# Two normalisation chains moved ahead in a three-engine schedule: GpSimd's second normalisation before its row DMAs, VectorE's and ScalarE's attention statistics, normalisation and residual before the low halves

## The chip, the cores and the metric

The kernel runs on one core of a Trainium2 chip. Its five engines (TensorE, VectorE, ScalarE, GpSimd and SyncE, in the profile PE, DVE, ACT, POOL and SP) each work through their own list of instructions in order, and are tied together by semaphores alone: an instruction that waits holds back all that is behind it on its engine. The metric is the device time of one execution in microseconds (us), the median of several runs; less is better.

## What is computed

One block of a sandwich network over x of shape (16, 1024, 256), float32: an attention-like gated recurrence, then a mixture of eight experts with a common overflow network. Both have a normalisation in front, one behind, and a residual sum. Cut to what matters:

```python
# first half, per sequence of 1024 tokens
n = layernorm(x)
g = sigmoid(n @ Wg.T + bg)
h_t = (1 - g_t) * h_(t-1) + g_t * n_t          # recurrence along the sequence
x = x + layernorm(h @ Wo.T + bo)
# second half, tokens of all sequences in one row
xf = layernorm(x)
eid = argmax(softmax(xf @ router_w + router_b))  # one of 8 experts
rank = how many earlier tokens chose the same expert
if rank < 320:  y = relu(xf @ w1[eid] + b1[eid]) @ w2[eid] + b2[eid]
else:           y = relu(xf @ ow1 + ob1) @ ow2 + ob2   # overflow network
x = x + layernorm(y)
```

## The kernel before

The 16,384 tokens are cut into 32 groups of 512 (NG = 32), two to a sequence; a group is named (i, v), with v = 0 or 1 its half. A loop of 32 steps runs over them, written as two steps u = 0 and u = 1 in a hardware loop, with the first and the last steps written out. It is a software pipeline. Step (i, u) works on `now`, for which it computes the routing and the overflow network (all tokens go through it), on `nxt`, the group after, for which it finishes the first half up to the transposed, normalised input of the second, and on `far`, the group after that, for which it does the first normalisation, the gate matmuls and the recurrence. Steps 0 to 30 have a `nxt`, steps 0 to 29 a `far`. Behind the loop eight experts are computed from rows that the steps scattered to DRAM (`xbuf`), 320 rows each; the change does not touch that part.

Matmuls are in float32 split into a high and a low half, three products for one: ScalarE makes the high half by a copy that rounds, VectorE (or GpSimd, for `hst_lo`) the low half by a subtraction. The hidden layer of 1024 is worked in eight slices j of 128. For each there are `layer1(j)` on TensorE (six matmuls into `psH`), `relu(j)` on ScalarE (the relu into `hid`, line 540, and the copy into `hid_hi`, line 544), `lo(j)` on VectorE (`hid_lo`, line 834), and `layer2(j)` on TensorE (twelve matmuls into `psY`). `low(j)` in VectorE's step is `lo(now, j)`, and `hidden(range)` in ScalarE's step is `relu` for those j.

The order of each engine within a step is written out by hand. TensorE's (lines 1116 to 1146) is: layer1(0), route, layer1(1), logits; project(nxt); layer1(2), layer2(0); layer1(3), layer2(1), transposes0(far); layer1(4), rank(now), layer2(2); layer1(5), layer2(3), **gate(far)**; layer1(6), layer2(4); layer1(7), layer2(5); **transposes1(nxt)**; layer2(6), layer2(7). The other engines' steps of before are in the listing below; their pieces are:

- `attended(nxt)` (VectorE, line 753) takes the projection out of PSUM into `att`. `stats1` takes its mean and variance (`read_rows`, four bn_stats, line 701, and `moments`, four bn_aggr, line 708, and two small tensor_scalar instructions, lines 712 and 713). `deviation(1)` on GpSimd makes `rstd` and `nmr` of them (lines 362 and 364), `norm1` on ScalarE normalises `att` in place (line 550), and `residual1` on VectorE adds x and writes `x1` (line 769).
- `stats2(nxt)` takes mean and variance of `x1`, `norm2` on GpSimd (with its `deviation(2)`) writes the normalised `tok2` (line 403, shown as tok), and `transposes1` on TensorE (line 1065) turns it into `psT`, from which `xf_hi` and `xf_lo` make the input of the next step.
- `choose(now)` finds the expert of each token from the logits. `rank(now)` on TensorE counts earlier tokens with the same expert, into `ranks`, which lies in `psA`; `place(now)` on VectorE (lines 816 to 829) turns that into a row number, `idx`, and signals `s_idx`; `dispatch(now)` on GpSimd issues four indirect DMAs (line 383) that write the rows of `x1` to `xbuf`.
- `norm0(far)` (GpSimd, tok, line 373), `transposes0`, `xn_hi` (ScalarE) and `xn_lo` (VectorE, line 734) make the input of the gate matmuls; `sigmoid(far)` and `recurrence(far)` follow them.
- `residual2(prev)` on GpSimd (line 438) is the last sum of the group before, 128x1024 in one instruction; SyncE stores it.

The gate matmuls write `psA`. Their waits, on TensorE, are on both halves of their input, on `attended(nxt)`, and on the row numbers of the group two before `far`, which is `now`:

```python
def gate(g):
    pe.wait_ge(s_xn_hi, cnt(g, 2, 2))
    pe.wait_ge(s_xn_lo, cnt(g, 2, 2))
    ...
    prev = grp(g[0], g[1], -2)
    if live(prev, NG):
        pe.wait_ge(s_idx, cnt(prev, 1, 1))
```

Of the kernel before, what the change touches and what calls it, by code (L numbers as in the profile page):

```python
# [14 lines left out]
D = 256  # L15
# [5 lines left out]
TG = 4  # L21
# [15 lines left out]
def cnt(g, n, k):  # L37
    return g[0] * (2 * n) + (g[1] * n + k)
# [8 lines left out]
def live(g, n):  # L47
    return not isinstance(g[0], int) or 0 <= 2 * g[0] + g[1] < n


def sandwich_kernel(nc, x, Wg, bg, Wo, bo, router_w, router_b, w1, b1, w2, b2, ow1, ob1, ow2, ob2, out):
    B, L, _ = x.shape
    N = B * L
    NG = N // GT
# [3 lines left out]
    with ExitStack() as ctx:  # L58
# [56 lines left out]
        x1 = [sb(f"x1_{v}", [P, TG, PITCH]) for v in range(2)]  # L115
# [79 lines left out]
        s_x1 = sem("s_x1")  # L195
# [143 lines left out]
        def _(pool):  # L339
# [47 lines left out]
            def renumber(g):  # L387

                i, v = g
                if live(grp(i, v, -2), NG):  # L390
                    pool.wait_ge(s_scat[v], landed(grp(i, v, -2), TG))
                    pool.sem_inc(s_held, 1)
                    pool.tensor_scalar(x1[v][:, :, D:ROW], x1[v][:, :, D:ROW], float(2 * GT), None, ALU.add)\
                        .then_inc(s_id, 1)

            def norm2(g, src, n, base=0):
                i, v = g
                deviation(2, g, n, base)
                pool.wait_ge(s_nm[2], cnt(g, 1, 1) + base)
                pool.wait_ge(s_T1, cnt(g, 2, 0) + 2 * base)  # L400
                pool.sem_inc(s_held, 1)
                for t in range(n):
                    last = pool.tensor_scalar(tok2[:, t, :], src[v][:, t, 0:D], rstd[2][:, t:t + 1],  # L403
                                              nmr[2][:, t:t + 1], ALU.mult, ALU.add)
                last.then_inc(s_tok2, 1)
# [9 lines left out]
            def step(i, u):  # L415
                prev, now, nxt, far = grp(i, u, -1), grp(i, u, 0), grp(i, u, 1), grp(i, u, 2)
                if live(prev, NG):
                    deviation(3, prev, TG)
                if live(far, NG):
                    norm0(far)  # L420
                if live(prev, NG):
                    residual2(prev)
                if live(nxt, NG):
                    deviation(1, nxt, TG)
                    renumber(nxt)
                if live(now, NG):
                    dispatch(now, range(TG))
                if live(nxt, NG):
                    norm2(nxt, x1, TG)
                if live(far, NG):  # L430
                    state_lo(far)

# [93 lines left out]
        def _(act):  # L526
# [19 lines left out]
            def norm1(g):  # L546
                act.wait_ge(s_nm[1], cnt(g, 1, 1))
                act.wait_ge(s_att, cnt(g, 2, 2))
                for t in range(TG):
                    last = act.activation(att[:, t, :], att[:, t, :], ACT.Identity, bias=nmr[1][:, t:t + 1],  # L550
                                          scale=rstd[1][:, t:t + 1])
                last.then_inc(s_u, 1)
# [53 lines left out]
            def step(i, u):  # L606
                now, nxt, far = grp(i, u, 0), grp(i, u, 1), grp(i, u, 2)
                run, up, ahead = live(now, NG), live(nxt, NG), live(far, NG)

                def hidden(js):  # L610
                    if run:
                        for j in js:
                            relu(now, j, GT, biasT[:, OB1 + j:OB1 + j + 1])

                hidden(range(0, 1))
                if run:
                    logits_out(now)
                hidden(range(1, 2))
                if live(grp(i, u, -1), NG):
                    norm3(grp(i, u, -1), TG)  # L620
                hidden(range(2, 4))
                if ahead:
                    xn_hi(far)
                hidden(range(4, 5))
                if up:
                    norm1(nxt)
                if not ahead:
                    for j in range(4 * u, 4 * u + 4):
                        weights_hi((0, 0), j)
                hidden(range(5, 6))  # L630
                if ahead:
                    sigmoid(far)
                hidden(range(6, 8))
                if up:
                    xf_hi(nxt, GT)
                if ahead:
                    state_hi(far)
# [56 lines left out]
        def _(dve):  # L694
# [21 lines left out]
            def stats(k, src, g, n, base=0):  # L716

                read_rows(k, src, n)
                moments(k, g, n, base)
# [39 lines left out]
            def stats1(g):  # L759
                dve.wait_ge(s_att, cnt(g, 2, 2))  # L760
                stats(1, lambda t: att[:, t, :], g, TG)

            def residual1(g):
# [4 lines left out]
                dve.wait_ge(s_u, cnt(g, 1, 1))  # L768
                dve.tensor_tensor(x1[v][:, :, 0:D], att[:], xin[v][:], ALU.add).then_inc(s_x1, 1)

            def stats2(g):
                dve.wait_ge(s_x1, cnt(g, 1, 1))
                stats(2, lambda t: x1[g[1]][:, t, 0:D], g, TG)

            def xf_lo(g, n, base=0):
                for c in range(DC):
# [92 lines left out]
            def step(i, u):  # L869
                now, nxt, far = grp(i, u, 0), grp(i, u, 1), grp(i, u, 2)  # L870
                run, up, ahead = live(now, NG), live(nxt, NG), live(far, NG)

                def low(*js):
                    if run:
                        for j in js:
                            lo(now, j, GT)

                low(0, 1)
                if run:
                    choose(now)  # L880
                if up:
                    attended(nxt)
                low(2)
                if up:
                    stats1(nxt)
                low(3)
                if ahead:
                    xn_lo(far)
                if run:
                    place(now)  # L890
                low(4)
                if up:
                    residual1(nxt)
                    stats2(nxt)
                low(5)
                if ahead:
                    recurrence(far)
                else:
                    for j in range(4 * u, 4 * u + 4):
                        weights_lo((0, 0), j)  # L900
                low(6)
                next_x = grp(i, u, 3)
                if live(next_x, NG):
                    read_rows0(next_x)
                low(7)
                if up:
                    xf_lo(nxt, GT)
                if live(next_x, NG):
                    moments(0, next_x, TG)
                if run and not up:  # L910
                    read_rows2((0, 0))
                    moments(2, (0, 0), ET, NG)
                if run:
                    result(now, ob2_b[:].unsqueeze(1), TG)
                if run and not up:
                    xf_lo((0, 0), C, NG)
                if run:
                    stats3(now, TG)
# [292 lines left out]
```

## Time and profile before

| | us |
|---|---|
| median of 3 runs | 1307.19 |
| lowest and highest run | 1305.34, 1312.45 |
| span of the profiled execution | 1305.6 |
| the profiled execution's own time beside its span | not given by the page |
| mean granted clock of TensorE over the span (share of 2.4 GHz) | 0.971 |

The first step starts at about 51.5 us and the last ends at about 1142 us; ahead of them lies the preparation of the weights, behind them the experts. A profile row gives the engine and the line of the kernel that issued the instruction, what it writes and reads, and its duration; in a timeline the first number is the start in us and the second the time to the end of the last of the merged instructions, and a bracket gives the idle time of the engine ahead of it and what ended that. Two instructions of one engine can overlap by some tenths of a microsecond, since they are pipelined.

### The profile page before, as it was taken

To read this page: it belongs to the slowest core of one execution; us is meant where nothing else is said; L and a number is where in the kernel's file an instruction comes from. 1 tells how busy PE (TensorE), PEld (TensorE's weight loads), DVE (VectorE), ACT (ScalarE), POOL (GpSimd) and SP (SyncE) were. 2 spreads that over 40 slices of the span, in tenths; PEclk is the share of its full clock that TensorE was granted. 3 is DMA by queue.
4 is the path that set the end of the run, shared out by engine and by line. 5 is a ranking of instruction groups with operands and counts; after the bars stand their busy time and mean duration, and the time that the engine had idled before them with its cause. 6 is when DMAs were issued, how large, how long until landed. Compare 5 with 4: busy or idle time off the path is not lost. (4 is left out here: it accounts for less than half of the span.)

```text
span 1305.6 us, 24820 instructions
## 1 busy us (share of the span) xinstructions
PE 1182.1 (91%) x7705; PEld 1048.7 (80%) x7705; DVE 1005.7 (77%) x2731; ACT 773.7 (59%) x1362; POOL 807.3 (62%) x887
## 2 busy tenths in 40 slices
PE   5599999999999999999999999999999999889994
PEld 4388888888888888888888888888888888789994
DVE  5678888887788878787888788787878776578892
ACT  4366566665656656665655556656655565467773
POOL 4466666666666666666666666656666665336774
PEclk9799999999999999999999999999999999989997
DMA  8211111111011010110111100101010100334430
GB/s 235 81 34 49 50 46 43 39 35 32 32 32 32 32 32 32 32 32 16 32 32 32 32 22 27 32 32 32 32 32 32 32 16 18 101 102 152 144 119 31
DMA packets 59687, 65.32 MB, mean 50 GB/s; under 512 B 7835, under 2 KB 55885, under 8 KB 59524
## 3 DMA queue, kind: packets, MB, share of 16 engines
q1 hardware_dynamic: 52484, 59.58, 14.6%
q0 software_dynamic: 7168, 5.32, 1.3%
q8 instruction: 16, 0.26, 0.1%
q14 instruction: 19, 0.16, 0.0%
HBM read 40.17 MB, written 38.87 MB: 61 GB/s over the span
## 5 line engine op out<-in xcount | busy, mean ns | idle before, releaser
L540 ACT ACTIVATE hid<-psH,biasT 128x512 f32<-128x512 f32 (+1 forms) x320 | 209.4, 654 | 281.0 <-PE psH L1011 257.8
L362 POOL TENSOR_TENSOR rstd<-veps,mhalf 128x4 f32<-128x4 f32 (+1 forms) x144 | 193.2, 1342 | 266.6 <-DVE nmean L713 266.3
L1109 PE MATMUL psY<-W_hi,hid_hi 128*128 128x256 f32 x1216 | 355.4, 292 | 0.9 <-DVE hid_lo L834 0.9
L1111 PE MATMUL psY<-W_lo,hid_hi 128*128 128x256 f32 x1216 | 348.0, 286 | 0.0
L1112 PE MATMUL psY<-W_hi,hid_lo 128*128 128x256 f32 x1216 | 347.9, 286 | 0.0
L834 DVE TENSOR_TENSOR hid_lo<-hid,hid_hi 128x512 fp32r<-128x512 f32 (+1 forms) x320 | 262.7, 821 | 99.1 <-ACT hid_hi L544 93.6
L1009 PE MATMUL psH<-xfT_hi,W_hi 128*128 128x512 f32 (+1 forms) x640 | 246.0, 384 | 6.2 <-ACT hid L540 3.4
L1109 PEld LDWEIGHTS psY<-W_hi,hid_hi 128*128 128x128 f32 x1216 | 235.1, 193 | 10.5 <-DVE hid_lo L834 1.8
L1011 PE MATMUL psH<-xfT_hi,W_lo 128*128 128x512 f32 (+1 forms) x640 | 242.7, 379 | 0.0
L1010 PE MATMUL psH<-xfT_lo,W_hi 128*128 128x512 f32 (+1 forms) x640 | 242.4, 379 | 0.0
L1111 PEld LDWEIGHTS psY<-W_lo,hid_hi 128*128 128x128 f32 x1216 | 234.3, 193 | 6.7
L1112 PEld LDWEIGHTS psY<-W_hi,hid_lo 128*128 128x128 f32 x1216 | 234.1, 192 | 0.0
L544 ACT ACTIVATE hid_hi<-hid 128x512 fp32r<-128x512 f32 (+1 forms) x320 | 192.2, 601 | 10.2
L383 POOL DMA_INDIRECT xbuf<-x,idx x128 | 140.9, 1101 | 89.8 <-DVE idx L829 55.0
L1009 PEld LDWEIGHTS psH<-xfT_hi,W_hi 128*128 128x128 f32 x640 | 121.8, 190 | 24.8 <-ACT hid L540 4.2
L1011 PEld LDWEIGHTS psH<-xfT_hi,W_lo 128*128 128x128 f32 x640 | 121.6, 190 | 22.5
L412 POOL TENSOR_TENSOR hst_lo<-hst,hst_hi 128x512 fp32r<-128x512 f32 x64 | 82.1, 1304 | 85.9 <-ACT hst_hi L582 85.9
L1010 PEld LDWEIGHTS psH<-xfT_lo,W_hi 128*128 128x128 f32 x640 | 121.9, 190 | 14.5
L1065 PE MATMUL psT<-ident,tok 128*128 128x128 f32 x304 | 46.8, 302 | 82.8 <-POOL tok L403 82.8
L1065 PEld LDWEIGHTS psT<-ident,tok 128*128 128x128 f32 x304 | 36.3, 151 | 91.0 <-POOL tok L403 89.3
L589 ACT ACTIVATE xfT_hi<-psT 128x512 fp32r<-128x512 f32 (+1 forms) x80 | 41.8, 562 | 106.6 <-PE psT L1065 106.5
L778 DVE TENSOR_TENSOR xfT_lo<-psT,xfT_hi 128x512 fp32r<-128x512 f32 (+1 forms) x80 | 49.1, 645 | 68.7 <-ACT xfT_hi L589 68.1
(110 smaller groups left out, 2290.6 us busy)
## 6 DMA issues: line engine op xcount, KB each, us to landing
xin<-L_attn_x SPq DMA_DIRECT2D x32, 512.0 KB
stage<-L_ffn_w SPq DMA_DIRECT2D x16, 1024.0 KB, 6.3
out<-outt SPq DMA_DIRECT2D x32, 512.0 KB, 2.9
xbuf<-zrow SPq DMA_DIRECT2D x1, 2570.0 KB, 17.7
xin<-xbuf SPq DMA_DIRECT2D x8, 257.0 KB, 5.7
stage<-L_ffn_ow SPq DMA_DIRECT2D x2, 1024.0 KB, 10.8
xbuf<-x,idx POOLq DMA_INDIRECT x128
b_b<-L_ffn_b SPq DMA_DIRECT2D x1, 1024.0 KB, 14.1
```

The costliest lines, as they stand in the source:

```text
L362: pool.tensor_tensor(rstd[k][:, 0:n], veps[k][:, 0:n], mhalf[:, 0:n], ALU.pow).then_inc(s_rs[k], 1)
L383: pool.indirect_dma_start(out=xbuf, out_offset=bass.IndirectOffsetOnAxis(idx[v][:, t:t + 1], 0), in_=x1[v][:, t, 0:ROW], in_offset=None, b ...
L540: act.activation(hid[j % 2][:, 0:n], psH[:, j % 2, 0:n], ACT.Relu, bias=bias).then_inc(s_hid, 1)
L544: act.activation(hid_hi[j % 4][:, 0:n], hid[j % 2][:, 0:n], ACT.Copy).then_inc(s_hid_hi, 1)
L834: dve.tensor_tensor(hid_lo[j % 4][:, 0:n], hid[j % 2][:, 0:n], hid_hi[j % 4][:, 0:n].bitcast(F32), ALU.subtract).then_inc(s_hid_lo, 1)
L1009: pe.matmul(dst, w_hi, r_hi, start=(k == 0), stop=False)
L1010: pe.matmul(dst, w_hi, r_lo, start=False, stop=False)
L1011: return pe.matmul(dst, w_lo, r_hi, start=False, stop=(k == last_k))
L1065: last = pe.transpose(psT[:, c, t * P:(t + 1) * P], tok2[:, t, c * P:(c + 1) * P], ident[:])
L1109: pe.matmul(psY_t[:, t, :], hi, w[0][:, j, :], start=(j == 0 and t % 2 == 0), stop=False, skip_group_check=True)
L1111: pe.matmul(psY_t[:, t, :], hi, w[1][:, j, :], start=False, stop=False, skip_group_check=True)
L1112: last = pe.matmul(psY_t[:, t, :], lo_, w[0][:, j, :], start=False, stop=(j == HC - 1), skip_group_check=True)
```

## The change

GpSimd's step computes `norm2(nxt)` before `dispatch(now)`. ScalarE's step runs `norm1(nxt)` ahead of `xn_hi(far)` and relu 4, not behind them. VectorE's step takes the attention statistics before low(2), then low(2) and low(3), then `residual1` and the four bn_stats of `x1`, then `xn_lo(far)`, then the moments of `x1`, low(4) and low(5), and only then `place(now)`. `stats2` is split into `read_rows2a` and `moments` so that `xn_lo` can stand between. TensorE's and SyncE's orders are as they were.

```diff
--- before.py
+++ after.py
@@ -423,10 +423,9 @@
                 if live(nxt, NG):
                     deviation(1, nxt, TG)
                     renumber(nxt)
+                    norm2(nxt, x1, TG)
                 if live(now, NG):
                     dispatch(now, range(TG))
-                if live(nxt, NG):
-                    norm2(nxt, x1, TG)
                 if live(far, NG):
                     state_lo(far)
 
@@ -619,11 +618,11 @@
                 if live(grp(i, u, -1), NG):
                     norm3(grp(i, u, -1), TG)
                 hidden(range(2, 4))
+                if up:
+                    norm1(nxt)
                 if ahead:
                     xn_hi(far)
                 hidden(range(4, 5))
-                if up:
-                    norm1(nxt)
                 if not ahead:
                     for j in range(4 * u, 4 * u + 4):
                         weights_hi((0, 0), j)
@@ -768,9 +767,13 @@
                 dve.wait_ge(s_u, cnt(g, 1, 1))
                 dve.tensor_tensor(x1[v][:, :, 0:D], att[:], xin[v][:], ALU.add).then_inc(s_x1, 1)
 
+            def read_rows2a(g):
+                dve.wait_ge(s_x1, cnt(g, 1, 1))
+                read_rows(2, lambda t: x1[g[1]][:, t, 0:D], TG)
+
             def stats2(g):
-                dve.wait_ge(s_x1, cnt(g, 1, 1))
-                stats(2, lambda t: x1[g[1]][:, t, 0:D], g, TG)
+                read_rows2a(g)
+                moments(2, g, TG)
 
             def xf_lo(g, n, base=0):
                 for c in range(DC):
@@ -880,19 +883,18 @@
                     choose(now)
                 if up:
                     attended(nxt)
-                low(2)
+                    stats1(nxt)
+                low(2, 3)
                 if up:
-                    stats1(nxt)
-                low(3)
+                    residual1(nxt)
+                    read_rows2a(nxt)
                 if ahead:
                     xn_lo(far)
+                if up:
+                    moments(2, nxt, TG)
+                low(4, 5)
                 if run:
                     place(now)
-                low(4)
-                if up:
-                    residual1(nxt)
-                    stats2(nxt)
-                low(5)
                 if ahead:
                     recurrence(far)
                 else:
```

## Rows read from the trace of the kernel before

**Rows 1.** The page, part 1: busy time, share, instructions.

```profile
PE 1182.1 (91%) x7705; PEld 1048.7 (80%) x7705; DVE 1005.7 (77%) x2731; ACT 773.7 (59%) x1362; POOL 807.3 (62%) x887
```

**Rows 2.** TensorE's waits, 60 to 1110 us: total, times, longest (us).

```profile
PE psT L1065 <- POOL tok L403: 60.7, 31, 3.2
```

**Rows 3.** Windows, logits copy to logits copy: length, busy PE, PEld, DVE, ACT, POOL, clock, DMA.

```profile
566.88:602.39 35.51, 33.41 (x211) 29.53 (x210) 27.89 (x77) 20.67 (x37) 22.42 (x24) 0.95 0.09 30
602.39:635.89 33.50, 31.86 (x211) 27.97 (x210) 26.96 (x77) 20.44 (x36) 21.71 (x24) 1.00 0.11 31
635.89:669.87 33.98, 31.87 (x211) 27.98 (x210) 27.74 (x77) 20.56 (x37) 22.46 (x24) 1.00 0.10 31
```

**Rows 4.** Timeline, TensorE, the second transposes: start, duration, instruction, [wait].

```profile
150.79 1.86 PE L1065 MATMUL psT<-ident,tok 128*128 128x128 f32 x8 [1.91 <-POOL tok L403]
...
629.25 1.09 PE L1065 MATMUL psT<-ident,tok 128*128 128x128 f32 x8 [1.64 <-POOL tok L403]
...
1003.74 1.50 PE L1065 MATMUL psT<-ident,tok 128*128 128x128 f32 x8 [2.10 <-POOL tok L403]
...
1140.18 1.54 PE L1065 MATMUL psT<-ident,tok 128*128 128x128 f32 x6 [4.94 <-POOL tok L403]
```

**Rows 5.** Timeline, GpSimd, 599 to 667 us.

```profile
608.44 2.38 POOL L438 TENSOR_TENSOR outt<-ysb,x 128x1024 f32<-128x1024 f32 x1
...
615.12 0.63 POOL L364 TENSOR_TENSOR nmr<-nmean,rstd 128x4 f32<-128x4 f32 x1
...
623.29 1.84 POOL L362 TENSOR_TENSOR rstd<-veps,mhalf 128x4 f32<-128x4 f32 x1
...
642.72 2.41 POOL L438 TENSOR_TENSOR outt<-ysb,x 128x1024 f32<-128x1024 f32 x1
```

**Rows 6.** Timeline, TensorE, around the gate matmuls of two steps.

```profile
617.35 0.39 PE L1011 MATMUL psH<-xfT_hi,W_lo 128*128 128x512 f32 x1
...
619.01 0.39 PE L1009 MATMUL psA<-xnT_hi,WgT_hi 128*128 128x512 f32 x1
...
652.40 0.29 PE L1112 MATMUL psY<-W_hi,hid_lo 128*128 128x256 f32 x1
652.52 0.39 PE L1009 MATMUL psA<-xnT_hi,WgT_hi 128*128 128x512 f32 x1
```

**Rows 7.** Timeline, VectorE, 599 to 667 us.

```profile
606.96 1.27 DVE L756 TENSOR_TENSOR att<-psA,bo_b 128x512 f32<-128x512 f32 x2
...
609.60 1.77 DVE L834 TENSOR_TENSOR hid_lo<-hid,hid_hi 128x512 fp32r<-128x512 f32 x1 [1.37 <-ACT hid_hi L544]
...
613.41 0.16 DVE L713 TENSOR_SCALAR nmean<-mv 128x4 f32<-128x4 f32 x1
...
621.74 0.69 DVE L834 TENSOR_TENSOR hid_lo<-hid,hid_hi 128x512 fp32r<-128x512 f32 x1
...
648.40 1.29 DVE L734 TENSOR_TENSOR xnT_lo<-xnT,xnT_hi 128x512 fp32r<-128x512 f32 x2
```

**Rows 8.** Timeline, ScalarE, 599 to 667 us.

```profile
616.12 2.07 ACT L550 ACTIVATE att<-att,nmr,rstd 128x256 f32<-128x256 f32 x4
...
626.23 0.69 ACT L540 ACTIVATE hid<-psH,biasT 128x512 f32<-128x512 f32 x1 [1.47 <-PE psH L1011]
626.95 0.63 ACT L544 ACTIVATE hid_hi<-hid 128x512 fp32r<-128x512 f32 x1
```

**Rows 9.** Timeline, VectorE, the last step.

```profile
1122.52 0.18 DVE L816 TENSOR_TENSOR rk<-psA,row 128x32 f32<-128x32 f32 x1
...
1123.62 0.17 DVE L829 CAST idx<-slot 128x4 int32<-128x4 f32 x1
...
1127.01 0.69 DVE L834 TENSOR_TENSOR hid_lo<-hid,hid_hi 128x512 fp32r<-128x512 f32 x1 [2.62 <-ACT hid_hi L544]
```

**Rows 10.** Timeline, all engines, 606 to 609 us.

```profile
606.27 2.20 POOL L373 TENSOR_SCALAR tok<-xin,rstd,nmr 128x256 f32<-128x256 f32 x4 [0.29 <-POOL nmr L364]
...
606.34 0.23 DVE L797 SCALAR_TENSOR_TENSOR cand<-lg,first 128x32 f32<-128x32 f32 x1
```

## Prediction

> **What bounds the kernel now.** I read the page's busy shares first, then the waits of TensorE, then the busy time of single steps, then the timeline of two neighbouring steps engine by engine. TensorE is busy 91% of the span, well ahead of VectorE's 77% [rows 1]. From the first step to the last that prepares another group, the trace shows TensorE waiting for one thing only: 31 times for the second normalised tile `tok2`, 60.7 us in all, 1.96 us each [rows 2]. Single steps show the same. Measured from one copy of the logits to the next, TensorE is busy 31.87 us in every step at the full clock; the rest is that wait, 1.63 us in a step with u=0 and 2.11 us in one with u=1 [rows 3]. So a step costs 31.87 us plus TensorE's waits. A third term is in the first of these rows: after some of the 2.1 us waits the clock falls to the lower of its two levels (1.2 instead of 2.4 GHz) for a while, the mean of the step is 0.95, and the same matmuls take 33.41 us, 1.54 us more. Seven of the 16 waits of 1.9 to 2.2 us are followed by this, the first at 150.79 and the last at 1003.74; of the 13 of 1.6 us, as at 629.25, none is [rows 4].
>
> **What the change removes.** GpSimd now computes `tok2` ahead of the four row DMAs, and VectorE has the statistics for it ready earlier. In the step that begins at 599.55 GpSimd starts on it at 623.29, behind the DMAs [rows 5], and TensorE's wait ends at 629.25 [rows 4], 6 us later. In the new order the statistics are there at about 619.8 (below) and nothing of GpSimd's is in front, so `tok2` is done by 625.8; TensorE wants it at 627.6 and, by what follows, later. I take the 31 waits as gone: -60.7 us.
>
> **What it adds: a wait of TensorE in front of the gate matmuls.** `gate(far)` waits on `s_idx` of the present group (line 1033), since it overwrites the PSUM in which `place(now)` reads the ranks. Up to now `place` ran before `low(4)`, and the gate started without a wait, at 619.01 and at 652.52 [rows 6]. The change puts `place` behind `low(5)`, and moves the attention statistics, the whole of `residual1`, the second statistics and `xn_lo` in front of it too. Everything that TensorE still has for this step (layer 1 for j=6 and 7, layer 2 from j=4, the transposes, the next step) is queued behind the gate. So I work out when `place` ends.
>
> First the start of `norm1` on ScalarE. `attended` ends at 608.23. Four statistics and the moments follow; now they run from 611.3, behind `low(2)`, to 613.57, 2.3 us [rows 7], which gives 610.5. But the two small tensor_scalar instructions at their end fall under GpSimd's residual addition, 2.38 us from 608.44, and a VectorE instruction with this kind of access is held by it: `low(2)` took 1.77 us, more than twice the 0.69 us of `low(5)`, and finished 0.55 us after the addition [rows 5, 7]. So the moments end at 611.05. From there to the end of GpSimd's nmr the present chain takes 613.57 to 615.75, 2.2 us, 0.63 of it an nmr with a VectorE `xn_lo` beside it [rows 5, 7]; I take 2.0. `norm1` starts at 613.1. With u=1 the residual addition runs from 642.72 to 645.13 [rows 5], later in its step by 0.8 us; the moments end at 645.4 and `norm1` starts at 647.45.
>
> Then from `norm1` to the end of `place`. From the start of `norm1` through `residual1` and the second statistics to the VectorE instruction behind them the trace has 616.12 to 621.74, 5.62 us [rows 7, 8]; no slack lies in it, since each waits for the one before. In the new order the two `xn_lo` (1.29 us [rows 7]) stand inside this stretch; they hide the 0.16 us between statistics and moments, so about 1.05 us more: 6.7. `low(4)` and `low(5)` follow back to back, 1.2 us for both (two `xn_lo`, of the same shape, take 1.29 with the pipeline's end). Their inputs come later than now, since `norm1` and `xn_hi` are ahead of relu 4 on ScalarE: 613.1 plus some 2 us for each of the two and two pairs of 1.3 us give 619.7, just in time. `place` takes 1.27 us (1122.52 to 1123.79 [rows 9]). Sum: 6.7 + 1.2 + 1.3 = 9.2 us.
>
> So the gate starts at 622.3 instead of 619.01, 3.3 us late, and with u=1 at 656.7 instead of 652.52, 4.15 us late. The last matmul before it ends 0.17 us after the gate could start (652.40 + 0.29 against 652.52 [rows 6]), so idle time as the rows count it is 3.15 and 4.0 us, mean 3.56. 30 steps have a gate: +106.8 us. Against -60.7 that is **+46 us**.
>
> **The last step.** There `place` moves from 1122.5 to behind `low(5)`, which ends at 1127.7 [rows 9], so the last row DMAs start 5.2 us later. The reload of the rows, the expert's normalisation and the transposes, for which TensorE waits 4.94 us already [rows 4], all follow from them: **+5 us**.
>
> **The clock.** None of the waits of 1.6 us is followed by a fall, seven of 16 near 2 us are, and the one of 4.94 us too: the six transposes behind it, started at 1140.18, took 1.54 us, and the eight of 629.25 took 1.09 us [rows 4]. So waits of 3 to 4 us should meet it more often than those of 2. I take 20 of the 30, seven being there already: 13 x 1.54 = **+20 us**. The bounds are no more than now (0) and every step (+35).
>
> **Sum**: 1305.6 + 46 + 5 + 20 = 1377. The page gives the profiled execution's span and no other time of it; the span lies 1.6 us below the median of 1307.2, so I forecast 1378 us.
>
> **VectorE beside GpSimd.** The cost I can bound least is what GpSimd's second normalisation does to `low(4)`, `low(5)` and `place`, with which it now coincides. The long two-input addition holds VectorE [rows 5, 7]. The normalisations don't seem to: `cand` (two inputs in SBUF) took 0.23 us under GpSimd's `tok` [rows 10], against 0.18 us for `rk`, of the same size with one of its inputs in PSUM [rows 9]. I take nothing; the bound above is one wait of half an instruction of `tok` (2.2 us for four [rows 10]) for each of some seven small instructions, 2 us a step, 60 us.
> By the Trainium skill (SBUF — State Buffer, Who interferes with whom) a VectorE instruction with two SBUF inputs and a GpSimd one that reads SBUF exclude each other, and the second is blocked until the first is done. `low(4)`, `low(5)` and three of `place`'s (lines 820, 821 and 823) are such instructions, and GpSimd's `tok` reads SBUF; the rule would bring the sum near the upper bound. The row of `low(2)` agrees with it for the long addition, the row of `cand` does not for `tok`.
>
> **Rivals.**
> 1. Only what can't be avoided is paid. `place` cannot start before `low(5)`: layer 1 for j=5 ends at 617.74 [rows 6], relu and copy take 1.35 us [rows 8], `low(5)` 0.69, `place` 1.27, so the gate starts at 621.1 at the earliest, with 1.95 us idle. That is what is removed (1.96): 30 x 1.95 - 60.7 + 5 = +3, so 1310, with the clock as now. It needs VectorE to be 1.2 to 2 us ahead of my chain, and the chain is made of rows without slack. Chance 0.05.
> 2. Faster. The same floor, and no wait of it is followed by a fall of the clock: 1307 + 3 - 11 = 1299. It decides when all waits stay under about 1.9 us, above which the trace first shows a fall. As the floor itself is 1.95, chance 0.04.
> 3. The gate wait as worked out, but the clock falls no more often than now, or the moments are not held by the addition: 1350 to 1362. In my own range; chance 0.2.
> 4. VectorE is held by the normalisation in small pieces, 0.5 to 2 us a step: 1395 to 1438. For it: the addition of [rows 5]; against it: [rows 10]. Chance 0.14.
> 5. The transposes still wait: `tok2` is ready at 624.5 and TensorE comes at 630.8, so this would take 6 us that I don't see. Chance 0.02.
> The forecast itself, 1362 to 1395, has the rest, 0.55.
>
> **How the numbers follow.** Within 0.5% (6.5 us), about what a measurement of this kernel can tell from no change, is rival 1: 0.05. Faster is rival 2: 0.04. Slower is the rest: 0.91. The range leaves out rivals 1 and 2 and the upper half of rival 4: 1345 to 1412. Its ends are also the sum with the gate wait 0.5 us shorter and few more falls, and the sum with every step's clock falling and 0.6 us of contention.
>
> **What would show it.** In the profile after: no wait of the transposes (line 1065) for `tok`; in its place one of the gate matmuls on `psA` (line 1009) for `idx` of line 829, 30 times, 3 to 4 us, longer with u=1; TensorE busy 31.87 us in a step at full clock; more steps with a clock below 1.00; `norm1` starting some 3 us earlier in the step; `place` last before the recurrence. The prediction is wrong if the gate starts without a wait, if the wait is near 2 us (VectorE ahead of my chain) or above 4.5 us (VectorE held), or if the clock stays at 1.00 through such waits.

## The result and the profile after

The changed kernel takes 1394.2 us (median of 4 runs, 1392.9 to 1397.4) beside 1306.8 us for the kernel before: 1.0665 times as long, 95% interval 1.0638 to 1.0692. It is slower by 87 us, inside the range given and 16 us above the time predicted. Executions of one kernel beside each other agree within 0.8% here, but for one of eight of the kernel with `place` two low halves earlier (1645.6 us, at a mean granted clock of 0.654) and the longer of the two with GpSimd's part undone (1463.8 us), and neither of these enters a ratio.

The page after: busy time and share of each engine.

```profile
PE 1218.2 (87%) x7705; PEld 1073.6 (77%) x7705; DVE 991.7 (71%) x2731; ACT 769.7 (55%) x1362; POOL 756.9 (54%) x887
```

TensorE's share has fallen from 91 to 87% [rows 1], although it is busy 36 us longer with the same 7705 matmuls. Its waits from 60 to 1200 us are these (total, times, longest), where the kernel before had 60.7 us for `tok` alone [rows 2]:

```profile
PE psA L1011 <- DVE idx L832: 107.6, 30, 4.1
PE psT L1067 <- POOL tok L403: 1.7, 1, 1.7
```

The wait for `tok2` is gone but for one step, and a wait of the gate matmuls for `idx` stands in its place, 30 times, 3.6 us on the mean. Three steps, again from one copy of the logits to the next (length; busy PE, PEld, DVE, ACT, POOL; granted clock; DMA):

```profile
280.75:315.97 35.22, 31.89 (x211) 28.04 (x210) 26.21 (x77) 20.42 (x37) 21.16 (x24) 1.00 0.10 32
536.62:573.90 37.28, 33.41 (x211) 29.14 (x210) 27.38 (x77) 20.40 (x36) 20.27 (x24) 0.95 0.09 28
573.90:611.61 37.71, 34.40 (x211) 29.94 (x210) 26.43 (x77) 20.40 (x36) 20.59 (x24) 0.91 0.08 28
```

The first is one of the four steps with a gate in which the clock stays at its upper level: 31.89 us busy, as before [rows 3], and 3.33 us of waiting. The second has one stretch at the lower level and costs 1.52 us more in matmuls. The third has a mean clock of 0.91 and costs 2.5 us more; before, no step went under 0.95. TensorE's timeline around its gate:

```profile
590.41 0.29 PE L1114 MATMUL psY<-W_hi,hid_lo 128*128 128x256 f32 x1
594.01 0.77 PE L1011 MATMUL psA<-xnT_hi,WgT_hi 128*128 128x512 f32 x1 [3.31 <-DVE idx L832]
594.57 0.63 PE L1012 MATMUL psA<-xnT_lo,WgT_hi 128*128 128x512 f32 x1
595.00 0.63 PE L1013 MATMUL psA<-xnT_hi,WgT_lo 128*128 128x512 f32 x1
```

The last matmul in front starts at 590.41, and the gate 3.6 us later. In [rows 6] these two are 0.12 us apart. Two gate matmuls behind it are 0.43 us apart, where at the upper level they are 0.23 us apart: the clock was already down when the wait ended. Half-microsecond windows of TensorE show from when to when (busy time, count, granted clock), here in the step with 0.91 and below it in the one with 0.95:

```profile
592.50:593.00 0.50, 0.00 (x0) 0.72 0.00 0
593.00:593.50 0.50, 0.00 (x0) 0.50 0.00 0
599.00:599.50 0.50, 0.50 (x3) 0.50 0.01 0
599.50:600.00 0.50, 0.50 (x3) 0.96 0.00 0
```

```profile
558.00:558.50 0.50, 0.50 (x3) 1.00 0.00 0
558.50:559.00 0.50, 0.50 (x3) 0.58 0.00 0
561.50:562.00 0.50, 0.50 (x3) 0.51 0.00 0
562.00:562.50 0.50, 0.50 (x4) 1.00 0.06 1
```

In the first the clock is down from 592.7 to 599.5, 6.8 us, 5.5 of them with work; in the second, whose wait ended at 557.3, it falls behind the wait, at 558.6, and is back after 3.4 us.

VectorE, GpSimd and ScalarE in the same step, which begins at 571.06:

```profile
581.78 0.61 DVE L711 TENSOR_SCALAR veps<-mv 128x4 f32<-128x4 f32 x1
...
586.98 1.23 DVE L768 TENSOR_TENSOR x<-att,xin 128x1024 f32<-128x1024 f32 x1 [2.35 <-ACT att L549]
...
589.56 1.28 DVE L733 TENSOR_TENSOR xnT_lo<-xnT,xnT_hi 128x512 fp32r<-128x512 f32 x2
...
591.38 1.29 DVE L837 TENSOR_TENSOR hid_lo<-hid,hid_hi 128x512 fp32r<-128x512 f32 x2
592.59 0.18 DVE L819 TENSOR_TENSOR rk<-psA,row 128x32 f32<-128x32 f32 x1
...
593.69 0.17 DVE L832 CAST idx<-slot 128x4 int32<-128x4 f32 x1
```

```profile
579.98 2.38 POOL L437 TENSOR_TENSOR outt<-ysb,x 128x1024 f32<-128x1024 f32 x1
...
591.56 1.41 POOL L362 TENSOR_TENSOR rstd<-veps,mhalf 128x4 f32<-128x4 f32 x1 [6.55 <-DVE nmean L712]
...
593.56 2.17 POOL L403 TENSOR_SCALAR tok<-x,rstd,nmr 128x256 f32<-128x256 f32 x4 [0.29 <-POOL nmr L364]
```

```profile
584.80 2.08 ACT L549 ACTIVATE att<-att,nmr,rstd 128x256 f32<-128x256 f32 x4 [0.90 <-POOL nmr L364]
```

This is the chain of the prediction, link by link, in a step with u=0. The residual addition (579.98, 2.38 us) holds the small tensor_scalar of the attention moments (0.61 us for 0.17); `norm1` starts at 584.80; `residual1` at 586.98, `xn_lo` at 589.56, low(4) and low(5) at 591.38, `place` at 592.59. Its last instruction ends at 593.86 and the gate starts at 594.01. In a step with u=1 that last instruction falls under GpSimd's `tok`, which starts at 556.56 there, and takes 0.40 us instead of 0.17 us, in all 15 of them:

```profile
556.74 0.40 DVE L832 CAST idx<-slot 128x4 int32<-128x4 f32 x1
```

Behind the steps, the transposes for the first expert wait 9.48 us, where they waited 4.94 us [rows 4]:

```profile
1228.74 1.54 PE L1067 MATMUL psT<-ident,tok 128*128 128x128 f32 x6 [9.48 <-POOL tok L403]
```

### The profile page after: what moved, and what is told of

It is laid out like the page before. It is cut to its first block and busy times, and to the rows that moved or that the text cites. A ratio compares the mean times of both kernels' runs of the same rounds, so it can differ in the third digit from the quotient of the medians.

```text
span 1395.7 us, 24833 instructions
## 1 busy us (share of the span) xinstructions
PE 1218.2 (87%) x7705; PEld 1073.6 (77%) x7705; DVE 991.7 (71%) x2731; ACT 769.7 (55%) x1362; POOL 756.9 (54%) x887
## 5 line engine op out<-in xcount | busy, mean ns | idle before, releaser
L362 POOL TENSOR_TENSOR rstd<-veps,mhalf 128x4 f32<-128x4 f32 (+1 forms) x144 | 179.2, 1245 | 375.4 <-DVE nmean L712 375.4
L1111 PE MATMUL psY<-W_hi,hid_hi 128*128 128x256 f32 x1216 | 350.3, 288 | 1.2 <-DVE hid_lo L837 1.2
L837 DVE TENSOR_TENSOR hid_lo<-hid,hid_hi 128x512 fp32r<-128x512 f32 (+1 forms) x320 | 210.4, 666 | 96.5 <-ACT hid_hi L543 88.7
L1111 PEld LDWEIGHTS psY<-W_hi,hid_hi 128*128 128x128 f32 x1216 | 230.1, 189 | 10.3 <-DVE hid_lo L837 1.9
L1113 PEld LDWEIGHTS psY<-W_lo,hid_hi 128*128 128x128 f32 x1216 | 229.9, 189 | 6.6
L383 POOL DMA_INDIRECT xbuf<-x,idx x128 | 146.2, 1143 | 44.2 <-issue 35.8
L1011 PE MATMUL psA<-xnT_hi,WgT_hi 128*128 128x512 f32 x128 | 71.5, 558 | 110.7 <-DVE idx L832 107.6
L573 ACT ACTIVATE keep<-psA,neg_bg 128x512 f32<-128x512 f32 x64 | 43.9, 688 | 208.2 <-PE psA L1013 208.2
L1011 PEld LDWEIGHTS psA<-xnT_hi,WgT_hi 128*128 128x128 f32 x128 | 33.7, 263 | 124.1 <-issue 116.9
L743 DVE SCALAR_TENSOR_TENSOR xnT<-keep,xnT 128x512 f32<-128x512 f32 x64 | 44.1, 689 | 110.6 <-ACT keep L573 110.2
## 6 DMA issues: line engine op xcount, KB each, us to landing
xbuf<-zrow SPq DMA_DIRECT2D x1, 2570.0 KB, 19.1
b_b<-L_ffn_b SPq DMA_DIRECT2D x1, 1024.0 KB, 14.4
```

Of the source, the lines that this page charges most:

```text
L362: pool.tensor_tensor(rstd[k][:, 0:n], veps[k][:, 0:n], mhalf[:, 0:n], ALU.pow).then_inc(s_rs[k], 1)
L383: pool.indirect_dma_start(out=xbuf, out_offset=bass.IndirectOffsetOnAxis(idx[v][:, t:t + 1], 0), in_=x1[v][:, t, 0:ROW], in_offset=None, b ...
L837: dve.tensor_tensor(hid_lo[j % 4][:, 0:n], hid[j % 2][:, 0:n], hid_hi[j % 4][:, 0:n].bitcast(F32), ALU.subtract).then_inc(s_hid_lo, 1)
L1011: pe.matmul(dst, w_hi, r_hi, start=(k == 0), stop=False)
L1111: pe.matmul(psY_t[:, t, :], hi, w[0][:, j, :], start=(j == 0 and t % 2 == 0), stop=False, skip_group_check=True)
L1113: pe.matmul(psY_t[:, t, :], hi, w[1][:, j, :], start=False, stop=False, skip_group_check=True)
```

## The experiments

Each kernel was timed beside the kernel before on the same chip. A ratio is to that kernel, with its 95% interval. Its median lay between 1306.1 and 1311.4 us from round to round, so a difference in microseconds between kernels of two rounds is good to about 5 us.

### Only `place` early again

The changed kernel with `place` where VectorE idles, ahead of `residual1`:

```diff
                 low(2, 3)
+                if run:
+                    place(now)
                 if up:
                     residual1(nxt)
...
                 low(4, 5)
-                if run:
-                    place(now)
```

> The changed kernel with one thing different: place(now) stands between low(3) and residual1, where VectorE idles (2.35 us in the step at 573.90), no longer behind low(5). Theory: the late place is the only thing that costs. TensorE's wait for idx (107.6 us) goes; what is left in front of the gate is xn_lo, which ends at 590.84 where the gate is due at 590.5, and moves 0.6 us with place: at most 1 us a step. No falls of the clock behind waits under 1.9 us. 1395.7 - 107.6 + 30 x (0.5 to 1) - 36 to 47 (clock) - 4.5 (last step) = 1255 to 1275 us, faster than before. Rival: the other moves (norm1 ahead of relu 4, the statistics ahead of the low halves) cost by themselves, by VectorE or ScalarE being late for layer 1 or the gate: TensorE then waits for xn_lo or for relu, and the time is 1300 us or more.

Measured: 1267.7 us, ratio 0.968 (0.965 to 0.970). One moved call turns a loss of 6.7% into a gain of 3.2%. TensorE's waits, then its gate and VectorE's `xn_lo` in one step:

```profile
PE psA L1011 <- issue: 30.0, 30, 1.1
```

```profile
568.84 0.47 PE L1011 MATMUL psA<-xnT_hi,WgT_hi 128*128 128x512 f32 x1 [0.97 <-issue]
```

```profile
567.47 1.28 DVE L733 TENSOR_TENSOR xnT_lo<-xnT,xnT_hi 128x512 fp32r<-128x512 f32 x2
```

The wait is 1.0 us a step and the profile names no releaser for it; `xn_lo` ends at 568.75 and the gate starts at 568.84, which points at the input as what is late now. The clock is at 1.00 in every step with a gate. The other moves of the change are not what costs.

### GpSimd's part alone

The kernel before with `norm2` ahead of `dispatch` and nothing else:

```diff
                     renumber(nxt)
+                    norm2(nxt, x1, TG)
                 if live(now, NG):
                     dispatch(now, range(TG))
-                if live(nxt, NG):
-                    norm2(nxt, x1, TG)
```

> The kernel before with GpSimd's part of the change alone: norm2 ahead of dispatch. Theory: this part is a pure gain. GpSimd starts on tok2 when the statistics end (621.83) and not behind the DMAs (623.29), and has fewer VectorE instructions beside it; TensorE's waits of 1.6 and 2.1 us fall to under 0.7 us, no clock falls: 1305.6 - 61 - 12 + 10 to 20 = 1242 to 1255 us. Rival: the DMAs, now last, hold hst_lo and the next step's first normalisations on GpSimd by 2 us, TensorE waits in project or VectorE is held later: 1270 to 1305 us. Second rival: VectorE's part of the change is needed for any gain: 1290 us or more.

Measured: 1269.7 us, ratio 0.969 (0.966 to 0.972), 15 us above what was expected and below the rival's 1270 by a hair. GpSimd's timeline and the transposes in one step:

```profile
604.62 1.41 POOL L362 TENSOR_TENSOR rstd<-veps,mhalf 128x4 f32<-128x4 f32 x1 [5.60 <-DVE nmean L712]
...
607.28 3.74 POOL L403 TENSOR_SCALAR tok<-x,rstd,nmr 128x256 f32<-128x256 f32 x4 [0.29 <-POOL nmr L364]
...
616.40 2.55 POOL L412 TENSOR_TENSOR hst_lo<-hst,hst_hi 128x512 fp32r<-128x512 f32 x2
```

```profile
611.07 1.09 PE L1064 MATMUL psT<-ident,tok 128*128 128x128 f32 x8 [0.95 <-POOL tok L403]
```

GpSimd is free when the statistics end, and the wait shrinks to 0.95 us, behind which the clock no longer falls. It doesn't shrink to nothing: `tok` takes 3.74 us for its four instructions beside VectorE's recurrence, where it took 2.2 us in [rows 10], and these 1.5 us are more than the wait. That its DMAs and `hst_lo` now run on into the next step (616.40) cost nothing that TensorE's waits show.

### GpSimd's part undone

The changed kernel with GpSimd's old order, `dispatch` ahead of `norm2`.

> The changed kernel with GpSimd's old order: dispatch ahead of norm2. Theory: dispatch waits for the late idx (593.86), its four DMAs end near 600.6, tok2 is ready near 606, where TensorE wants it at 602.4 to 604: waits of 2 to 4 us for tok2 come back beside the gate's wait, 1395 + 31 x 2 to 3.5 = 1455 to 1505 us. Rival: VectorE's earlier statistics make tok2 early enough in either order, 1396 us.

Measured: its two executions took 1426.5 and 1463.8 us, and the profiled one is the longer, so the rows below are the longer one's. The shorter is 32 us above the changed kernel and under the 1455 to 1505 us expected; the longer is inside. The mean clock is 0.924 in both, and what parts them is open. The rival's 1396 us is out either way. GpSimd and TensorE in one step:

```profile
625.71 1.12 POOL L383 DMA_INDIRECT xbuf<-x,idx  x1 [9.76 <-DVE idx L833]
...
633.68 2.60 POOL L403 TENSOR_SCALAR tok<-x,rstd,nmr 128x256 f32<-128x256 f32 x4 [0.30 <-POOL nmr L364]
```

```profile
636.33 1.09 PE L1068 MATMUL psT<-ident,tok 128*128 128x128 f32 x8 [1.16 <-POOL tok L403]
```

The first DMA waits 9.76 us for `idx`, `tok2` comes behind all four, and the transposes wait for it as they used to (34.3 us over 20 steps up to 1150 us), beside a gate wait that is as long as in the changed kernel with u=0 and 0.24 us shorter with u=1 (3.64 us). So GpSimd's swap is needed as soon as `place` is late; it is the good part of the change.

### `place` late and nothing else

The kernel before with `place` moved behind low(5):

```diff
-                if run:
-                    place(now)
                 low(4)
                 if up:
                     residual1(nxt)
                     stats2(nxt)
                 low(5)
+                if run:
+                    place(now)
```

> The kernel before with one thing of the change alone: place(now) behind low(5). Theory: this one move makes the gate's wait. low(5) ends at 622.35 in the step at 599.55, place 1.27 us later, the gate waits 4.5 us with u=0 and 4.7 us with u=1, 138 us in all; dispatch, now waiting for idx too, holds norm2 behind it on GpSimd, so that the transposes wait 2 to 3.7 us as well: 1305.6 + 138 + 0 to 50 + 40 (clock) + 5 = 1490 to 1540 us. Rival: the gate's wait came from the whole chain being moved together, and place alone costs little: under 1400 us.

Measured: 1481.4 us, ratio 1.134 (1.127 to 1.141), 9 us under the lower end expected.

```profile
PE psA L1009 <- DVE idx L829: 141.4, 30, 5.0
PE psT L1065 <- POOL tok L403: 24.3, 17, 2.2
```

141.4 us of gate waits, 4.7 us each, against 138 worked out. The wait for `tok2` is the smaller part that was overrated (24.3 us). This one move makes the loss by itself. The rest of the change takes some of it back: it brings the chain in front of `place` forward, and GpSimd's swap frees `tok2` of `dispatch`.

### `place` two low halves earlier

The changed kernel with `place` ahead of low(4) and low(5), still behind the moments.

> The changed kernel with place(now) ahead of low(4) and low(5), still behind the moments. Theory: the chain in front of place sets the gate's start one to one. The wait shortens by the two low halves, 1.2 us: 2.1 us with u=0, 2.65 us with u=1, 72 us in all where it was 107.6; at such waits the clock falls in half to most of the steps, 15 to 30 us less than in the changed kernel: 1395.7 - 36 - 15 to 30 = 1330 to 1345 us. Rival: relu 4 and 5 and their low halves set it (place is held by ScalarE's late copies), so the wait shortens by more than 1.2 us: under 1320 us; or something else holds the gate, and it stays near 3.5 us: 1385 us or more.

Measured: 1319.3 us, ratio 1.010 (1.007 to 1.013).

```profile
PE psA L1011 <- DVE idx L832: 68.0, 30, 2.7
```

The wait is 2.11 us with u=0 and 2.43 us with u=1, 68.0 us in all: shorter than in the changed kernel by 1.2 us, what the two low halves take, and by 1.45 us. The further 0.23 us with u=1 is the last instruction of `place`, which now ends ahead of GpSimd's `tok` and takes 0.17 us again in all steps. So the chain sets the gate's start one to one. The time is 11 to 26 us less than expected, just under the 1320 us of the rival, but the waits are those of the theory. The clock fell in 7 steps only, not in half of them, so that TensorE is busy 37 us less than in the changed kernel and not 15 to 30 (1181.4 against 1218.2 us), and the transposes of the last step wait 4.5 us instead of 9.48, which was left out of the sum.

### The wait filled with work

The changed kernel with 14 further matmuls ahead of the gate's wait. They compute nothing that is used.

```diff
                 if live(prev, NG):
+                    for _ in range(14):
+                        pe.matmul(psA[:, 0, :], W1[1][0][:, 0, 0:P], xfT_hi[:, 0, :], start=True, stop=True)
                     pe.wait_ge(s_idx, cnt(prev, 1, 1))
```

> The changed kernel with 14 further matmuls of 128x512 (14 x 0.233 = 3.27 us) ahead of the gate's wait for idx; they write the half of psA that the gate overwrites. Nothing else needs them. Theory: the wait sets the time and the fall of the clock is a consequence of TensorE idling in it. The gate starts when it did, idle time there is 0 to 0.7 us a step, the clock stays at its upper level, and the 1.56 to 2.6 us a step of slower matmuls (48 us over the steps) go: 1345 to 1355 us, although TensorE has 98 us more work. Rival: the falls come from something else in the step: clock 0.95 as before, 1390 to 1400 us. Second rival: the added matmuls delay the gate beyond idx: above 1400 us.

Measured: 1353.1 us, ratio 1.033 (1.029 to 1.036). The added matmuls and the gate in one step, and two steps as windows:

```profile
607.01 3.50 PE L1036 MATMUL psA<-xfT_hi,W_hi 128*128 128x512 f32 x14 [0.47 <-issue]
610.35 0.48 PE L1011 MATMUL psA<-xnT_hi,WgT_hi 128*128 128x512 f32 x1
```

```profile
554.36:589.76 35.40, 35.15 (x225) 30.66 (x224) 26.25 (x77) 20.41 (x36) 20.11 (x24) 1.00 0.09 30
589.76:625.43 35.67, 35.20 (x225) 30.58 (x224) 27.18 (x77) 20.40 (x37) 20.69 (x24) 1.00 0.09 29
```

The clock is at 1.00 in all steps with a gate, the steps take 35.4 and 35.7 us instead of 35.2 to 38.2, and the kernel is 41 us faster than the changed one with 420 matmuls more. So the idling is what brings the clock down. What is left over the kernel before is the wait itself, now filled.

### The gate one slice later

The changed kernel with one line of TensorE's order changed, so that layer1(6) and layer2(4) stand in front of the wait:

```diff
-                    if j == 5 and ahead:
+                    if j == 6 and ahead:
                         gate(far)
```

> The changed kernel with gate(far) on TensorE one slice later (behind layer1(6) and layer2(4), at j == 6). Theory: place may stay late if TensorE has 2.8 us of other work in front of the wait. The gate is due 22.3 us into the step and idx comes at 22.8 (u=0) and 23.4 us (u=1): idle 0.4 to 0.9 us, the clock stays at its upper level; low(6) and low(7) come 0.5 us late for layer 2 behind the later recurrence. 31.87 + 1 to 1.5 us a step, and the last step's 4.5 us: 1262 to 1285 us. Rival: the recurrence, started 3 us later against the rest, holds low(6), low(7) and hst_hi, and TensorE waits 2 to 3 us a step for them: 1300 us or more.

Measured: 1357.6 us, ratio 1.038 (1.033 to 1.044). The theory fell: the gate's wait is down to 8.6 us in all, even less than expected (0.4 to 0.9 us a step), but 70.9 us of waits for `hid_lo` took its place. VectorE, GpSimd and TensorE:

```profile
586.40 3.31 DVE L837 TENSOR_TENSOR hid_lo<-hid,hid_hi 128x512 fp32r<-128x512 f32 x1
```

```profile
586.65 2.50 POOL L412 TENSOR_TENSOR hst_lo<-hst,hst_hi 128x512 fp32r<-128x512 f32 x2
```

```profile
589.76 0.58 PE L1111 MATMUL psY<-W_hi,hid_hi 128*128 128x256 f32 x1 [2.86 <-DVE hid_lo L837]
```

The rival that stood against it named the recurrence. The rows name something else: low(7) takes 3.31 us, and GpSimd's two long subtractions of `hst_lo` now fall on it; layer 2 for j=7 waits 2.86 us for it. This is so in 14 steps, every second one.

### The same, with `place` early too

> Both: place(now) before residual1, and gate(far) at j == 6. Theory: in the kernel with place early TensorE still waits 1.0 us a step for xn_lo (30.0 us over 30 steps); with 2.8 us of other work in front this goes. What is left is what the later recurrence costs behind the gate, 0 to 0.7 us a step: 1266 - 30 + 0 to 20 = 1236 to 1256 us, the fastest so far. Rival: the tail behind the gate (recurrence, low(6), low(7), hst_hi) is the next bound and gives the 30 us back: 1262 to 1275 us.

Measured: 1414.7 us, ratio 1.082 (1.077 to 1.088), far from both forecasts. There is no wait at the gate at all, and this in its place:

```profile
PE psY L1111 <- DVE hid_lo L837: 114.8, 89, 2.9
```

Of the 30 steps with a gate 28 have one wait of 2.83 us or more for `hid_lo`, and in 28 low(7) takes 3.3 us, as at 577.92, where `hst_lo` (578.18 to 580.68) stands beside it; with the late `place` there were 14. The mean clock is under 1.00 in 27 of these 28 steps.

### low(7) out of the way of `hst_lo`

The kernel with the later gate, and on VectorE:

```diff
-                low(6)
+                low(6, 7)
                 next_x = grp(i, u, 3)
                 if live(next_x, NG):
                     read_rows0(next_x)
-                low(7)
```

> The kernel with gate(far) at j == 6, and on VectorE low(7) ahead of the four bn_stats of the next x (read_rows0), no longer behind them. In the run with the gate at j == 6 alone, low(7) started at 586.40, 0.25 us before GpSimd's hst_lo, and took 3.31 us; TensorE waited 2.86 us for it. Theory: VectorE's two-input low(7) is held by GpSimd's two long two-input instructions (hst_lo, 2.50 us). Placed 1.3 us earlier it takes 0.69 us as usual and layer 2 for j=7 finds it ready; what stays is 0.2 to 0.5 us for low(6) and for idx, and no falls of the clock: 31.87 + 0.5 to 1.2 us a step, 1255 to 1285 us. Rival: low(7) is late for another reason (its copy on ScalarE), or hst_lo now holds what stands next (xf_lo, which the next step's first matmuls wait for): 1320 us or more.

Measured: 1296.5 us, ratio 0.989 (0.987 to 0.992). VectorE and GpSimd:

```profile
588.32 1.27 DVE L837 TENSOR_TENSOR hid_lo<-hid,hid_hi 128x512 fp32r<-128x512 f32 x2
```

```profile
589.93 2.52 POOL L412 TENSOR_TENSOR hst_lo<-hst,hst_hi 128x512 fp32r<-128x512 f32 x2 [0.75 <-ACT hst_hi L581]
```

Both low halves take 1.27 us together and are done before GpSimd starts; the waits for `hid_lo` fall from 70.9 to 19.1 us and 61 us of time go. That shows the hold as the cause in the kernel with the later gate. For the one with both edits it was not tried. The time is 12 us above the upper end expected. Of that, 15 waits for `xfT_lo` are 3.8 us. Beside them TensorE is recorded busy 21 us longer than in the kernel with `place` early (1193.6 against 1172.6 us), with the same matmuls and the clock at 1.00 in every step: a matmul's record of 0.28 us runs on into a wait, where the next would have started after 0.12 us, so each of the many short waits costs more than its idle time. The forecast counted the idle time alone.

### Two versions built from this

The first is the changed kernel with `place` early and `xn_lo` ahead of the bn_stats of `x1`.

> The changed kernel with place before residual1 and xn_lo(far) ahead of the four bn_stats of x1. Theory: the 1.0 us that the gate still waited with place early was for xn_lo (ends at 568.75, gate 568.84); 1.3 us earlier, this wait goes, and tok2, which was ready at 577.0 for transposes at 577.3, becomes late by up to 1 us: 1267 - 30 + 0 to 30 = 1237 to 1267 us. Rival: the gate's 1.0 us was a wait for something else (the row numbers or the semaphore instructions themselves), and stays: 1266 to 1270 us.

Measured: 1247.8 us, ratio 0.955 (0.954 to 0.957). The gate's 1.0 us is gone, so it was for `xn_lo`.

The second starts from the kernel before:

```diff
 GpSimd:  norm2(nxt) ahead of dispatch(now), as in the change
 ScalarE:
                 if ahead:
                     xn_hi(far)
-                hidden(range(4, 5))
                 if up:
                     norm1(nxt)
+                hidden(range(4, 5))
 VectorE:
                     attended(nxt)
-                low(2)
-                if up:
                     stats1(nxt)
-                low(3)
+                low(2, 3)
                 if ahead:
                     xn_lo(far)
                 if run:
                     place(now)
-                low(4)
                 if up:
                     residual1(nxt)
                     stats2(nxt)
-                low(5)
+                low(4, 5)
```

> A version built from what the runs showed: the kernel before with norm2 ahead of dispatch; on ScalarE xn_hi(far), then norm1(nxt), then relu 4; on VectorE the attention statistics ahead of low(2), then low(3), xn_lo, place, residual1, the second statistics, low(4), low(5). So place and xn_lo stay early, for the gate, and the chain to tok2 is shorter. In the kernel with GpSimd's part alone TensorE waits 0.95 to 1.1 us a step for tok2, whose statistics end at 604.5; here norm1 no longer stands behind relu 4 and residual1 no longer behind low(4), which brings them to about 603.2, 1.3 us earlier. Theory: no wait of TensorE is left, steps of 31.9 to 32.3 us: 1268 - 31 x 0.6 to 1.05 = 1236 to 1250 us. Rival: GpSimd is now the next bound: its DMAs and hst_lo run into the next step, whose first rstd already waits only 0.2 us, so that the residual addition and with it the held VectorE instructions move later, and the gain is given back: 1258 to 1272 us.

Measured: 1243.5 us, ratio 0.953 (0.952 to 0.955): the lowest time of all, 5% under the kernel before and 11% under the changed one, though its interval touches that of the version before (0.954 to 0.957). The two largest waits of TensorE from 60 to 1250 us:

```profile
PE psT L1061 <- POOL tok L403: 12.2, 23, 5.0
PE psA L1005 <- POOL hst_lo L412: 3.7, 15, 0.4
```

A step takes 31.9 to 32.5 us, of which 31.9 are matmuls.

## Why the prediction was right, and where it was off

**The removal** (-60.7 us): right. One wait for `tok2` of 1.7 us is left, in step 30, which has no gate.

**The gate's wait** (+106.8 us): measured 107.6 us. Its links: `norm1` was put 13.55 us into a step with u=0 and came at 13.74 us; from there to the end of `place` 9.2 us were worked out and 9.06 us measured. With u=1 `norm1` was put at 14.4 us and came at 13.9 us, and from there to the end of `place` it took 9.43 us. The waits were forecast as 3.15 and 4.0 us and are 3.31 and 3.9 us. So each link is right to half a microsecond, and that the total is right to 1 us is luck in part, since the errors cancel. That `place` is the cause, and not the moves around it, is shown from both sides: putting it back alone gives 1267.7 us, moving it alone 1481.4 us. That its distance counts one to one is shown by the kernel with `place` two low halves earlier. The prediction gives two times for the end of `tok2`, 625.8 and, in rival 5, 624.5; it came 24.7 us into the step, which is 624.2 on that scale.

**The last step** (+5 us): measured 9.48 - 4.94 = 4.5 us.

**The clock** (+20 us): the mis-sized term. TensorE is busy 1218.2 us where it was busy 1182.1 us, +36 us. I took 20 falls at 1.54 us, 13 more than before. The windows of the 30 steps with a gate show a mean clock under 1.00 in 26: 18 of these near 0.95, with 1.55 us each, and eight at 0.91, with 2.2 to 2.6 us each. Less the seven falls of before that is the 36 us. So the number was too low, and the step that failed is the price: I took it from falls of one length, and in eight steps the clock stayed down for twice as long (6.8 us in the windows above). That is why 36 us lie above the +35 that I had called the bound, although four steps have no fall. The count was badly founded too: of the two waits of about 3 us that the kernel before has, at 1040.12 (2.93 us) and 1105.49 (3.15 us), only the second is followed by a fall, and I used neither. That this time is a consequence of the idling, and not of the moved work, is shown by the filled wait: 41 us less with more matmuls.

**Sum**: 107.6 + 1.7 - 60.7 + 4.5 + 36.1 = 89.2 of the 90.1 us between the two spans.

**VectorE beside GpSimd**, taken as nothing: nearly right, in part by the order of events. low(4) and low(5) took 1.29 us for both beside GpSimd's rstd, which took 1.41 us where it takes 1.01 us elsewhere, so GpSimd paid. With `tok`, for which the upper bound was worked out, `place` hardly coincides: with u=0 `tok` starts at 593.56, when only the last instruction of `place` is left, and with u=1 that instruction is held, by 0.23 us in each of 15 steps, 3.5 us in all, which lie in the 107.6. It takes 0.17 us in all steps with `place` early, with `place` two low halves earlier and with GpSimd's part undone. The rule of the Trainium skill (SBUF — State Buffer, Who interferes with whom) would have held `place` and brought the time near the upper bound, 1438 us. For `tok` these rows do not put it to the test, since none of the two-input instructions of `place` stands beside it, and rstd (591.56 to 592.97) did not hold low(5), which ended at 592.67. A hold as long as the GpSimd instruction is shown for the long ones: the tensor_scalar took 0.61 us and, in the experiment with the later gate, low(7) 3.31 us.

**The rivals**: the floor (1310 us) and the faster case (1299 us) did not occur, since the chain had no slack. Rival 3 is out, since the clock fell in 26 steps and the moments were held. Rival 4 is out by the rows and not by the time: 1394.2 us is 1 us under its lower end, and what brought it there is the clock. Rival 5 is out, with one wait of 1.7 us.

## What to carry to other kernels

Before a call is moved behind others on one engine, list who waits for its semaphore: `place` is 1.3 us of work that nothing on VectorE needed early, but the next matmuls of TensorE need its buffer, and each microsecond that it was moved back was a microsecond of TensorE per step. A wait of TensorE costs its length and, from about 2 us here, often a stretch of half speed behind it. Behind waits of 1.0 and 1.6 us there was none; whether several short waits cost less than one long one of the same total was not tried. When an order is changed, look again at where the long two-input instructions of GpSimd fall on VectorE: the kernel that removed every gate wait, with such a hold in its steps, was 108 us slower than the one before.

## What the runs showed of the hardware

- How often the clock falls with the length of the wait: none of 30 steps at 1.0 us, none of 13 at 1.6 us, 7 of 16 at 1.9 to 2.2 us; with `place` ahead of low(4) 3 of 12 at 2.1 us and 4 of 17 at 2.3 to 2.7 us; with the later gate 10 of 14 at 2.8 to 2.9 us; in the changed kernel 8 of 12 at 3.3 us and 17 of 17 at 3.7 to 4.1 us. So the length alone does not decide it below 3.7 us, and what else does stays open. Matmuls whose result nobody needs keep the clock up as well as others do.
- low(7) is recorded from 586.40 and GpSimd's `hst_lo` from 586.65 to 589.15, yet low(7) ends at 589.71: the instruction with the earlier start in the profile was the one held.
- VectorE held GpSimd's normalisation far more than the other way round: the four instructions of `tok` took 5.63 us beside VectorE's recurrence and low(6) in the kernel with `place` early, which was itself hardly slower (its two scans took 1.39 and 1.28 us, against 1.28 us each in the changed kernel), and 2.17 us in the changed one, where VectorE idled:

```profile
571.39 5.63 POOL L403 TENSOR_SCALAR tok<-x,rstd,nmr 128x256 f32<-128x256 f32 x4 [0.24 <-POOL nmr L364]
```
